# Both MLPs of a two-layer transformer block on one core: the activated chunk stays in its PSUM bank, with three banks for the wide product and one for the transposed tile

## The reference, cut to what matters

```python
    x = layer_norm(video + attn, g2, be2)
    ff = jax.nn.relu(x @ W1.T + b1) @ W2.T + b2
    return layer_norm(x + ff, g3, be3)
...
    h = (x - mu) * jax.lax.rsqrt(var + EPS) * ln_gamma + ln_beta
    y = jax.nn.silu(hf @ w1 + fc1_bias)
    z = y @ w2 + fc2_bias
    return residual + 0.5 * z.reshape(residual.shape)
```

## Time and profile before

| | |
|---|---|
| median of 3 runs | 2610.03 us (2608.24 to 2620.02) |
| the profiled execution | 2602.43 us, its span 2600.7 us |
| TensorE matmul busy | 2374.5 us, 91% of the span |
| VectorE busy | 1808.4 us, 70% |
| ScalarE busy | 1293.4 us, 50% |
| GpSimd busy | 704.3 us, 27% |
| `m` MLP, its wide products | 1804 to 2200 us |
| `d` MLP, its wide products | 2242 to 2589 us |

### The profile page before, as it was taken

The page is one execution under the profiler, slowest core; times in us unless marked ns, Lnnn a source line. Parts: engine busy times, 40 slices in busy tenths (PEclk is TensorE's granted clock), DMA queues, the critical chain, the costliest instruction groups (busy, mean ns, idle before and its releaser), DMA issues. The chain is left out here.

```text
span 2600.7 us, 43661 instructions
## 1 busy us (share of the span) xinstructions
PE 2374.5 (91%) x15960; PEld 2184.8 (84%) x15960; DVE 1808.4 (70%) x3357; ACT 1293.4 (50%) x2026; POOL 704.3 (27%) x468
## 2 busy tenths in 40 slices
PE   6988897799898887999999999998999999499999
PEld 6887886788888886988988988987999998399998
DVE  5666665899999975665665664665687785777774
ACT  4444443434434423554554564555667664355665
POOL 1111011444444442231131131123344441211111
PEclk9999998899999998999999999996999999699999
DMA  5000000000000000000000000002000010000000
GB/s 175 0 0 0 0 0 9 11 1 0 0 0 0 1 1 17 9 8 16 8 8 16 8 8 16 8 19 63 25 25 16 24 41 1 35 26 25 24 24 33
DMA packets 42971, 45.69 MB, mean 18 GB/s; under 512 B 3088, under 2 KB 41872, under 8 KB 42640
## 3 DMA queue, kind: packets, MB, share of 16 engines
q1 hardware_dynamic: 42896, 44.69, 5.3%
HBM read 27.90 MB, written 16.78 MB: 17 GB/s over the span
## 5 line engine op out<-in xcount | busy, mean ns | idle before, releaser
L1885 DVE TENSOR_TENSOR m_a_lo<-m_a,m_a_hi 128x512 fp32r<-128x512 f32 x128 | 124.4, 988 | 90.8 <-ACT m_a_hi L1844 90.8
L1840 ACT ACTIVATE d_a<-d_ps_wide,d_b,d_w_gain 128x512 f32<-128x512 f32 x128 | 99.8, 779 | 136.8 <-PE d_ps_wide L272 134.6
L1295 POOL TENSOR_TENSOR p_kf<-p_kf,p_k_shift 128x1024 f32<-128x1024 f32 x64 | 119.4, 1903 | 155.5 <-DVE p_k_shift L1430 155.5
L1797 PE MATMUL m_ps_z<-m_w_hi,m_a_hi 128*128 128x256 f32 x512 | 146.2, 286 | 0.0
L1797 PE MATMUL d_ps_z<-d_w_hi,d_a_hi 128*128 128x256 f32 x512 | 143.6, 280 | 1.0 <-DVE d_a_lo L1885 1.0
L1797 PE MATMUL m_ps_z<-m_w_hi,m_a_lo 128*128 128x256 f32 x512 | 144.2, 282 | 0.0
L1797 PE MATMUL m_ps_z<-m_w_lo,m_a_hi 128*128 128x256 f32 x512 | 144.1, 281 | 0.0
L1797 PE MATMUL d_ps_z<-d_w_lo,d_a_hi 128*128 128x256 f32 x512 | 143.4, 280 | 0.0
L1797 PE MATMUL d_ps_z<-d_w_hi,d_a_lo 128*128 128x256 f32 x512 | 142.6, 279 | 0.0
L1885 DVE TENSOR_TENSOR d_a_lo<-d_a,d_a_hi 128x512 fp32r<-128x512 f32 x128 | 85.8, 689 | 77.0 <-ACT d_a_hi L1844 72.5
L270 PE MATMUL f_ps_gate<-f_gate_w_hi,f_n_T_hi 128*128 128x352 f32 x256 | 94.4, 369 | 40.9 <-ACT f_silu L985 40.9
(11 more groups left out here) (361 smaller groups left out, 8557.8 us busy)
## 6 DMA issues: line engine op xcount, KB each, us to landing
residual<-in_x SPq DMA_DIRECT2D x8, 1024.0 KB, 11.8
attn<-p_attn SPq DMA_DIRECT2D x32, 256.0 KB, 2.2
m_attn<-attn SPq DMA_DIRECT2D x16, 512.0 KB, 3.8
out<-residual SPq DMA_DIRECT2D x16, 512.0 KB, 2.9
raw_weights<-in_d_q SPq DMA_DIRECT2D x2, 1024.0 KB, 7.2
d_scale<-in_d_scale SPq DMA_DIRECT2D x2, 1024.0 KB, 6.0
raw_weights<-in_m_w1T SPq DMA_DIRECT2D x1, 1024.0 KB, 5.0
raw_weights<-in_m_w2T SPq DMA_DIRECT2D x1, 1024.0 KB, 8.0
```

Source lines behind the costliest of these rows:

```text
L1295: pool.tensor_tensor(f, f, k_shift[:, i, :].unsqueeze(2).broadcast_to([P, HEADS, M]), ALU.subtract).then_inc(k_shifted, 1)
L1797: mm = pe.matmul(z, a, w[:, f, :], start=(f == 0 and k == 0 and j % 2 == 0), stop=(f == FC - 1 and k == 2), skip_group_check=True)
L1840: act.activation(self.a[f % RING][:, :], self.ps_wide[f % 2][:, :], self.func, bias=self.b1[:, f:f + 1], scale=gain(f))
L1885: dve.tensor_tensor(self.a2[1][:, f, :], self.a[f % RING][:, :], self.a2[0][:, f, :].bitcast(F32), ALU.subtract).then_inc(self.a_lo, 1)
```

## The change

The tile `a` in SBUF and its ring of four (`RING`) go. ScalarE first writes `a_hi` to SBUF and then applies the function to the bank in place, so the activated chunk lies in PSUM; VectorE's `split_a` reads it from there. A bank is therefore free only when `a_lo` of its chunk is made, and `widen` waits for that. `ps_n` shrinks to one bank, and `ps_wide` has three, chunk f in bank f % 3. A turn has eight chunks, so chunk 0 waits for chunk 6 of the turn before and chunk 1 for chunk 7, two chunks back; the others wait for the chunk three back, except chunk 2, which waits for chunk 5. The transposes are made in two halves, ahead of `widen(2)` and `widen(4)`, and `scale_n` of a half follows `activate(1)` and `activate(3)`. In the `m` MLP `normalise_x` moves from behind `activate(1)` and `activate(2)` to behind `activate(5)` and `activate(6)`.

```diff
-        self.a = [core.sbuf(f"{name}_a{s}", [P, BANK]) for s in range(RING)]
-        self.ps_n = core.psum(f"{name}_ps_n", [P, KD * BANK])
-        self.ps_wide = [core.psum(f"{name}_ps_wide{s}", [P, BANK]) for s in range(2)]
+        self.ps_n = core.psum(f"{name}_ps_n", [P, BANK])
+        self.ps_wide = [core.psum(f"{name}_ps_wide{s}", [P, BANK]) for s in range(WIDE_BANKS)]
...
+        def turn_n(c):
+            def phase(t, s):
+                if c == 0:
+                    pe.wait_ge(self.n_ready, t + 1)
+                wait_count(pe, self.h_ready, KD * t + c)
...
-                wait_count(pe, self.a_ready, FC * t + f - 1)
+                last = f - WIDE_BANKS if f >= WIDE_BANKS else f + (FC - 1 - f) // WIDE_BANKS * WIDE_BANKS - FC
+                wait_count(pe, self.a_lo, FC * t + last + 1)
...
-            if f == 2:
-                phases.append((self.N, turn_n))
+            if f in TURNS:
+                phases.append((self.N, turn_n(TURNS.index(f))))
...
-                wait_count(act, self.a_lo, FC * t + f + 1 - RING)
-                act.activation(self.a[f % RING][:, :], self.ps_wide[f % 2][:, :], self.func,
-                               bias=self.b1[:, f:f + 1], scale=gain(f))
-
                 wait_count(act, self.z_added, FC * (t - 1) + f + 1)
-                act.activation(self.a2[0][:, f, :], self.ps_wide[f % 2][:, :], self.func,
+                act.activation(self.a2[0][:, f, :], bank[:, :], self.func, bias=self.b1[:, f:f + 1], scale=gain(f))
+                act.activation(bank[:, :], bank[:, :], self.func,
                                bias=self.b1[:, f:f + 1], scale=gain(f)).then_inc(self.a_ready, 1)
...
-                dve.tensor_tensor(self.a2[1][:, f, :], self.a[f % RING][:, :], self.a2[0][:, f, :].bitcast(F32),
+                dve.tensor_tensor(self.a2[1][:, f, :], self.ps_wide[f % WIDE_BANKS][:, :], self.a2[0][:, f, :].bitcast(F32),
```

More of the change, by code:

```diff
@@ L1686 @@
 NM = T // GM
-RING = 4
+WIDE_BANKS = 3
 BEHIND = 4
+TURNS = [2, 4]
 class Mlp:
@@ L1755, in tensor @@
         ident = self.core.ident
[L1757 to L1760, removed]
+        def turn_n(c):
[3 more added lines that the diff above has]
+                wait_count(pe, self.h_ready, KD * t + c)
                 for j in range(GM):
-                    mm = pe.transpose(self.ps_n[:, c * BANK + j * P:c * BANK + (j + 1) * P],
-                                      self.n[s][:, j, c * P:(c + 1) * P], ident[:, :])
+                    mm = pe.transpose(self.ps_n[:, j * P:(j + 1) * P], self.n[s][:, j, c * P:(c + 1) * P], ident[:, :])
                 mm.then_inc(self.n_turned, 1)
+            return phase
         def widen(f):
@@ L1776, in phase @@
                     if c < self.whole:
-                        pe.matmul(self.ps_wide[f % 2][:, :], w[0], h[0], start=(c == 0), stop=False)
-                        mm = pe.matmul(self.ps_wide[f % 2][:, :], w[0], h[1], start=False, stop=(c == KD - 1))
+                        pe.matmul(self.ps_wide[f % WIDE_BANKS][:, :], w[0], h[0], start=(c == 0), stop=False)
+                        mm = pe.matmul(self.ps_wide[f % WIDE_BANKS][:, :], w[0], h[1], start=False, stop=(c == KD - 1))
                     else:
-                        mm = product(pe, self.ps_wide[f % 2][:, :], w, h, start=(c == 0), stop=(c == KD - 1))
+                        mm = product(pe, self.ps_wide[f % WIDE_BANKS][:, :], w, h, start=(c == 0), stop=(c == KD - 1))
                 mm.then_inc(self.wide_done, 1)
@@ L1827, in gain, with scale_n, phase @@
             return 1.0 if self.gain is None else self.gain[:, f:f + 1]
-        def scale_n(t, s):
-            for c in range(KD):
+        def scale_n(c):
+            def phase(t, s):
                 act.wait_ge(self.n_turned, KD * t + c + 1)
                 wait_count(act, self.h_lo, KD * (t - 1) + c + 1)
-                act.activation(self.h[:, c, :], self.ps_n[:, c * BANK:(c + 1) * BANK], ACT.Identity,
+                act.activation(self.h[:, c, :], self.ps_n[:, :], ACT.Identity,
                                scale=self.scale[:, c:c + 1], bias=self.shift[:, c:c + 1]).then_inc(self.h_ready, 1)
+            return phase
         def activate(f):
             def phase(t, s):
+                bank = self.ps_wide[f % WIDE_BANKS]
                 act.wait_ge(self.wide_done, FC * t + f + 1)
-                wait_count(act, self.a_lo, FC * t + f + 1 - RING)
-                act.activation(self.a[f % RING][:, :], self.ps_wide[f % 2][:, :], self.func,
-                               bias=self.b1[:, f:f + 1], scale=gain(f))
                 wait_count(act, self.z_added, FC * (t - 1) + f + 1)
-                act.activation(self.a2[0][:, f, :], self.ps_wide[f % 2][:, :], self.func,
+                act.activation(self.a2[0][:, f, :], bank[:, :], self.func, bias=self.b1[:, f:f + 1], scale=gain(f))
+                act.activation(bank[:, :], bank[:, :], self.func,
                                bias=self.b1[:, f:f + 1], scale=gain(f)).then_inc(self.a_ready, 1)
@@ L2121, in normalise_o @@
                 return phase
-            self.steps = mlp.scalar(act, beside=((0, 1, normalise_x(0, 1)), (0, 2, normalise_x(2, 3)), (1, 4, normalise_y(0, 1)),
-                                                 (1, 5, normalise_y(2, 3)), (mlp.Z, 6, normalise_o(0, 1)),
+            self.steps = mlp.scalar(act, beside=((1, 4, normalise_y(0, 1)), (1, 5, normalise_y(2, 3)), (0, 5, normalise_x(0, 1)),
+                                                 (0, 6, normalise_x(2, 3)), (mlp.Z, 6, normalise_o(0, 1)),
                                                  (mlp.Z, 7, normalise_o(2, 3))))
```

4 lines of the change are left out of this document (2 added, 2 removed).

## The result

The changed kernel takes 2621.68 us, the median of 14 runs (2616.48 to 2626.88), and the kernel before, beside it on the same chip, 2605.83 us (14 runs, 2601.65 to 2620.02). The ratio is 1.0057, with a 95% interval of 1.0043 to 1.0071: slower by 15 us, 11 to 19 with the interval.

A forecast was written before the change was run, and what follows sets the result against it. Both MLPs were taken to run at the pace of TensorE's matmuls, so only TensorE's waits count. 1.3 + 7.1 + 2.6 + 3.3 + 2.0 = 16.3 us on 2610.0 gave 2626.3 us, range 2612 to 2640.

The forecast's parts named there:

- What bounds the kernel: Both MLPs: TensorE's matmuls set the pace, so taking work or waits off ScalarE, VectorE or SBUF gains 0.
- The loop in the `d` MLP: `d` MLP: TensorE waits on VectorE's list every turn, 22.00 us against 21.41, 0.59 us in 12 turns, 7.1 us.
- The tightest place: `d` turn: chunk 0 waits for chunk 6's low part of the turn before, 0.42 us late, plus 0.17 us release.
- Split transposes: Two halves pay the slow first matmul twice: 0.09 us in each of 14 `m` turns, 1.3 us; hidden in `d`.
- The last full turn: End of `d`: a GpSimd collision delays `split_h` and chunk 4's low part, so chunk 7 starts later: 2.6 us.
- The first full step: Start of `d`: chunk 6 waits some 4 us for chunk 3's late low part, delaying the next turn by 3.3 us.
- the clock: Start of `d`: after TensorE's standstill the granted clock falls to 1.2 GHz; bounds 0 and 2.5 us, taken as 2.0.
- ScalarE in place, VectorE from PSUM: ScalarE's in-place write, bounded by -2.6 and +2.6 us, taken as 0; VectorE's low part as fast from PSUM, 691 ns.
- The estimate of 0.4 us a turn: `d` loop: six low parts reading PSUM would add 0.4 us a turn, 5 us in all; left out of the sum.
- The rival by which the kernel gains: Both MLPs: matmuls speed up once ScalarE no longer writes `a` to SBUF, 22 us gained, 2604 us; chance 0.05.
- The `m` MLP: `m` turns: chunk 7's low part comes 0.6 us earlier, in time for chunk 1; taken as 0, upper end 5 us.
- the two ends: `d` MLP: the delays in its first full step, 3.3 us, and its last full turn, 2.6 us.

The follow-up runs named there:

- the run with the `d` MLP alone: Changed kernel with the `m` MLP put back to its old form, so only the `d` MLP is new; 2616.96 us, ratio 1.0042 to the kernel before.
- the run with the low parts early: Changed kernel, VectorE's `d` list reordered: statistics first; in the first full step, chunks 0, 1 and 3's low parts moved ahead; 2616.54 us, ratio 1.0041.
- the extra addition behind chunk 4: Changed kernel with one more 128 x 512 VectorE addition per `d` turn, between chunk 4's low part and `take_z`; `d` turn 22.50 us.
- the addition at the head: Changed kernel with one more 128 x 512 VectorE addition per `d` turn, first in VectorE's list; `d` turn 21.91 us.

## Why the prediction was right

The direction, the size (0.62% more forecast, 0.57% measured) and the mechanism held. By its steps:

**What bounds the kernel: right.** VectorE's work stayed and its collisions in `m` went (2.889 us at most before, 0.694 after), and that alone brought nothing: with `m` alone in the new form the ratio is 0.9993.

**The loop in the `d` MLP: right in kind, too large by 0.13 us a turn.** Forecast 22.00, measured 21.87. The terms in the turn above: from chunk 0's start (2438.84) to chunk 1's low part (2444.39) 5.55 us, where the forecast has 5.48 plus 0.11 for the slow start of the block; from that low part to the end of chunk 6's 2438.77 - 2422.47 = 16.30 against 16.35; 0.06 as forecast. Together 21.91, and turns alternate between 21.9 and 21.8. So 12 turns cost 5.5 us and not 7.1. The shorter activation in place is 0.03 of it.

**The tightest place: incomplete.** The prediction named chunk 0, with chunk 7 near its limit, and gave chunk 1 room. It did not look at chunk 6, whose bank waits for chunk 3's low part. In the trace chunks 6, 7 and 0 wait in a row. It cost no more than forecast, since all three are behind the same list; whether another order would make chunk 6 the tight one, no run shows.

**Split transposes: wrong in sign.** Forecast +0.09 us a turn in `m`, measured -0.08, and 0 in `d`. The extra slow first matmul is there; eight transposes with it took 0.79 + 0.09 us, and two times four take 2 x 0.35 + 2 x 0.09 = 0.88, the same sum. For the transposes start 0.109 us apart, but the wide matmul starts 0.03 us behind the last of a block: what a block of transposes gains at its end, 0.08 us, it loses behind the next matmul. The step that failed was to count that loss once more for the second block and not that gain. Why `m` gains on top, I can only say where: the blocks of `narrow` behind the split transposes take 1.36 and 1.38 us where 1.41 is usual.

**The last full turn: right.** Forecast 2.6, measured 23.74 - 21.41 = 2.3 us, by the collision named. GpSimd, VectorE (the split of `h`, blocked, and chunk 4's low part) and TensorE's chunk 7:

```profile
2564.24 2.39 POOL L2231 TENSOR_TENSOR residual<-residual,d_b 128x1024 f32<-128x1024 f32 x1 [3.02 <-DVE residual L2280]
```

```profile
2564.67 2.23 DVE L1879 CAST d_h_hi<-d_h 128x512 fp32r<-128x512 f32 x1
...
2568.61 0.68 DVE L1888 TENSOR_TENSOR d_a_lo<-d_ps_wide,d_a_hi 128x512 fp32r<-128x512 f32 x1
```

```profile
2569.35 0.50 PE L1781 MATMUL d_ps_wide<-d_h_hi,d_w_hi 128*128 128x512 f32 x1 [1.70 <-DVE d_a_lo L1888]
```

**The first full step: the standstill's sum nearly fits, its story and the clock do not.** Forecast 3.3 us (3.2 by its own numbers, 2272.9 - 2269.67) and 2.0 for the clock, measured 25.90 - 23.15 = 2.75 in all. The prediction had one standstill of 4 us ahead of chunk 6. There were two short ones, since chunk 3 already waits, for chunk 0's low part behind that of the weights; the prediction did not look at it:

```profile
2269.74 0.79 PE L1781 MATMUL d_ps_wide<-d_h_hi,d_w_hi 128*128 128x512 f32 x1 [1.31 <-DVE d_a_lo L1888]
```

```profile
2280.56 0.50 PE L1781 MATMUL d_ps_wide<-d_h_hi,d_w_hi 128*128 128x512 f32 x1 [1.55 <-DVE d_a_lo L1888]
```

```profile
2265.00:2272.00 7.00, 5.50 (x14) 3.95 (x15) 6.74 (x18) 3.36 (x5) 0.00 (x0) 0.50 0.00 0
2276.00:2280.00 4.00, 3.01 (x21) 2.58 (x20) 3.82 (x11) 1.91 (x3) 0.98 (x1) 1.00 0.00 0
2281.00:2286.00 5.00, 5.00 (x35) 4.50 (x34) 3.39 (x6) 2.67 (x4) 0.00 (x0) 1.00 0.02 3
```

The clock was already at its lower level when the step began, at the end of a wait of 5.3 us for the transposes, and it stayed at the upper one behind the 1.55 us. But it came back late: 9.5 us into the step, where before had it back after 4.7, and the blocks of chunks 3 and 4, with what follows each, took 1.4 us more for it. That 1.4 us came in place of standstill. In the run with the `d` MLP alone chunk 4's block is 0.83 us shorter, the wait ahead of chunk 6 is 0.83 us longer, and chunk 6 starts 31.49 us behind the first transposes of `d` in both:

```profile
2272.38 0.50 PE L1781 MATMUL d_ps_wide<-d_h_hi,d_w_hi 128*128 128x512 f32 x1 [2.38 <-DVE d_a_lo L1888]
```

VectorE is busy without a gap from the weights' low part to chunk 2's and waits then for its root alone, so its list sets that start, and on top of it the clock cost nothing; the term of 2.0 measured 0. That a standstill of the length I had in mind can cost is seen in the run with the low parts early: behind 3.62 us two blocks took 2.29 and 2.56 us, 2.3 more than usual. (In the earlier trace rows a mean of 0.71 over 4 us is the lower level for 58% of them, so it held for 4 + 0.58 x 4 = 6.3 us there, and not for some 5.)

**ScalarE in place, VectorE from PSUM: right.** Both taken at 0; measured -0.03 us and 0. The estimate of 0.4 us a turn, by which a rule of the Trainium skill (VectorE: DVE Perf Modes, section on the TRN2 errata) would have made the list longer, is in no run. The rival by which the kernel gains has no support either: wide matmuls that follow each other come 0.23 us apart before and after.

**The `m` MLP: right, with a small term missed.** No turn waits. But its first turns have a wait for a low part (0.5 us here, 1.8 in others) and one for `m_h` (0.9 us), and the second half of the first transposes of `d` waits 1.9 us for ScalarE, which has to empty the one bank first: 0.7 us more (16.11 against 15.39 to the next transposes). None of it was in the sum.

**Sum.** Forecast 1.3 + 7.1 + 2.6 + 3.3 + 2.0 = 16.3 us. Measured by the trace: 0.7 + 2.75 + 5.5 + 2.3 = 11.3 in `d` and 0.8 in and behind `m`, 12.1; with the longest `m` of the same code (370.31 us) and what follows it there, it would be 13.6. The ratio of the runs says 15 (11 to 19). Against the trace the sum is 4.2 us too high: the transposes by 2.3, the clock by 2.0, the loop by 1.6, the two ends by 0.9, less 2.6 us that were not in it (0.7 at the start of `d`, 1.9 in the first turns of `m` and behind it). So the forecast owes a part of its closeness to errors of both signs, and that part is luck.

## What to carry to other kernels

A buffer that is kept until a later engine has read it ties its refill to that engine's *list*, not to its load: VectorE was 37 of 50 us busy, and still an instruction of 0.61 us in front of the awaited low part cost TensorE 0.63 us a turn, and the same instruction at the head of the list 0.04. So write down, for every bank, which instruction frees it and what stands ahead of that in its list, for each step at the ends too; and if the residence is wanted, reorder the list in the same edit. A short wait behind a full pipeline is in no list of waits: compare the distance of one repeated instruction.

## What the hardware did that I had not expected

- GpSimd's power of 128 x 8 (the root for the normalisation) took 1.647 us beside a low part that reads one operand from PSUM, and 2.048 us when that low part read two from SBUF and had started 0.15 us ahead of it. In the kernel before, both are in SBUF too, but the power starts 0.06 us first and takes 1.65 us: in these rows who comes first decides.
- ScalarE wrote PSUM in 742 ns where the same activation into SBUF, as fp32r, took 772 (128 x 512, in `d`). The Trainium skill (ScalarE: Activation LUTs, Step-by-step: what each stage is for) says that PSUM is the faster destination; the rows agree, and put it at 30 ns.
- A standstill of TensorE of 3.62 us was followed by a granted clock of 0.50 for 5 us, and one of 1.55 us by 1.00. The length of the wait alone does not tell which: behind 2.03 us (the extra addition behind chunk 4) the clock was 0.50 for 3.4 us, and behind 2.38 us (the `d` MLP alone) and 2.31 us (the addition at the head) it was 1.00.
- The time up to the `m` MLP, in identical code, lay between 1785.7 and 1801.9 us in single profiles, 0.9% apart. For changes of half a per cent, two profiles can be compared part by part only.
